# Segment means packed densely by one-hot matmuls, and two stages with longer pipelines, in a four-layer graph network kernel

## The reference

```
h   = relu(layernorm(x))                                   # layer 0
msg = concat(h[src], edge_attr_128) @ W1 + b1
m   = segment_sum(msg, dst) / max(deg, 1)
o   = m + (m @ W2 + b2);  x1 = x + where(o >= 0, o, SLOPE * o)
x2  = layer 1: attention over the edges, segment softmax by dst, batch norm, feed-forward
x3  = x2 + layer 2: gate = edge_attr_32 @ W_edge, gated messages summed per destination or source
out = x3 + layer 3: one weight per edge type, mean per (dst, type), segment_sum
```

## Time and profile before

| what | value |
| --- | --- |
| median of 3 runs | 6724.53 us (6719.76 to 6727.48) |
| the profiled execution | 6720.99 us |
| its span | 6719.2 us |
| busy: GpSimd (POOL), VectorE (DVE), TensorE (PE), ScalarE (ACT) | 66%, 61%, 58%, 34% of the span |
| data moved by DMA | 872.41 MB, 130 GB/s over the span |

### The profile page before, as it was taken

One profiled execution on the slowest core, in us unless ns is written; L12 is line 12 of the kernel. 1 busy time (PEld: TensorE's weight loads), 2 busy tenths in 40 slices (PEclk: granted clock), 3 DMA queues, 4 the chain that ended last, 5 costly groups with the idle time before them and its releaser, 6 DMA issues. The chain is left out here.

```text
span 6719.2 us, 77949 instructions
## 1 busy us (share of the span) xinstructions
PE 3919.8 (58%) x14034; PEld 2340.2 (35%) x14034; DVE 4127.0 (61%) x11066; ACT 2269.6 (34%) x4611; POOL 4404.5 (66%) x3737
## 2 busy tenths in 40 slices
PE   1666664000577777658966667777720048788776
PEld 1444442000344444434445544444410013333332
DVE  7333333676688888674455566666659976666664
ACT  1333333333344344335556521111123332222222
POOL 2777776777677777600057756666665568888887
PEclk9777677555787788758977778888865568888888
DMA  7444444887222222195467755555546633333333
GB/s 225 118 122 123 127 131 142 268 261 248 66 55 59 60 64 65 56 401 173 153 220 231 227 141 102 104 102 101 104 117 212 213 108 43 43 44 43 43 43 37
DMA packets 767166, 872.41 MB, mean 130 GB/s; under 512 B 212895, under 2 KB 425587, under 8 KB 767105
## 3 DMA queue, kind: packets, MB, share of 16 engines
q1 hardware_dynamic: 440656, 453.86, 23.5%
q0 software_dynamic: 200704, 185.92, 15.4%
q10 hardware_dynamic: 125744, 231.99, 9.3%
HBM read 452.69 MB, written 464.35 MB: 136 GB/s over the span
## 5 line engine op out<-in xcount | busy, mean ns | idle before, releaser
L544 POOL DMA_INDIRECT at_first_table<-n_h,n_first_edge x784 | 811.7, 1035 | 826.2 <-ACT n_h L226 588.0
L552 POOL DMA_INDIRECT sum_table<-e_res,e_target x392 | 660.1, 1684 | 382.1 <-DMA sum_table<-e_res,e_target 116.7
L1961 PE MATMUL e_m<-e_by_rel,rel_w 128*128 128x512 f32 x1568 | 808.6, 675 | 0.0
L552 POOL DMA_INDIRECT out<-e_res,e_target x392 | 619.4, 1580 | 133.8 <-issue 107.5
L1090 PE MATMUL e_hs<-ident,e_hs 128*128 128x128 f32 x392 | 92.8, 380 | 825.4 <-DMA e_hs<-h_table,e_idx 825.4
L544 POOL DMA_INDIRECT att_table<-e_res,e_row x392 | 461.7, 1178 | 138.8 <-issue 138.8
L536 POOL DMA_INDIRECT e_x<-x,e_idx x392 | 379.4, 968 | 241.4 <-DMA e_idx<-idx 122.1
L536 POOL DMA_INDIRECT e_hs<-h_table,e_idx x392 | 410.0, 1046 | 131.7 <-issue 119.2
L1961 PEld LDWEIGHTS e_m<-e_by_rel,rel_w 128*128 128x128 f32 x1568 | 331.4, 217 | 427.0 <-issue 427.0
L1898 DVE SCALAR_TENSOR_TENSOR e_by_rel<-e_y,e_part_t 128x512 f32<-128x512 f32 x784 | 477.5, 680 | 0.0
L544 POOL DMA_INDIRECT mean_table<-e_res,e_row x392 | 390.6, 996 | 119.5 <-issue 107.0
(11 more groups left out here) (242 smaller groups left out, 10690.0 us busy)
## 6 DMA issues: line engine op xcount, KB each, us to landing
x_table<-n_x ACTq DMA_DIRECT2D x294, 256.0 KB, 3.0
e_hd<-at_first_table SPq DMA_DIRECT2D x196, 256.0 KB
n_x<-x_table SPq DMA_DIRECT2D x196, 256.0 KB
mean_table<-prep_zero ACTq DMA_DIRECT2D x1, 25284.0 KB
n_mean<-mean_table SPq DMA_DIRECT2D x98, 258.0 KB
e_edge<-edge128T SPq DMA_DIRECT2D x98, 256.0 KB
at_first_table<-e_zero SPq DMA_DIRECT2D x98, 256.0 KB, 2.1
gate_table<-e_gate ACTq DMA_DIRECT2D x98, 256.0 KB
```

Source lines behind the costliest of these rows:

```text
L544: pool.indirect_dma_start(out=table, out_offset=bass.IndirectOffsetOnAxis(ap=idx[:, t:t + 1], axis=0), in_=tile[:, t, :], in_offset=None, ...
L552: pool.indirect_dma_start(out=table, out_offset=bass.IndirectOffsetOnAxis(ap=idx[:, t:t + 1], axis=0), in_=tile[:, t, :], in_offset=None, ...
L1961: ins = pe.matmul(flat(at(ps_m, u - 1)), k.rel_w[:, r, :], at(by_rel, u - 1)[:, r, :], start=(r == 0), stop=(r == RELS - 1))
```

## The change

Layer 0's table of means is no longer indexed by node. Each run of equal `dst` has a number; the table `mean_runs` holds one row of 130 numbers for each run, in order: the mean, the first edge's position and the destination. In e0 a one-hot matrix (`pick`, made by comparing a run's place inside its half step with 1 to 256) is multiplied with the 512 rows of results, so that the last edge of each run lands at its run's row (`ps_c`); ScalarE copies the 512 packed rows out, and SyncE writes them by two plain DMAs of 256 rows at a row number that it reads from a table. Rows behind the last run are rubbish that the next write covers, so each of these writes waits until the one before has landed. The scatter by GpSimd, and the zeros in `mean`, are gone.

In n0, SyncE loads for each tile of 128 nodes the 128 rows of `mean_runs` that begin with the first run of that tile; VectorE compares each row's destination with the node numbers (`local`, `pick`), and four matmuls spread the rows to their nodes. `prepare` computes run numbers and row numbers (a small search with a gather), folds W2 + 1 into W1 and b1 (so L704 becomes a transposition), and rewrites the indices, since node tables now hold a step's rows in another order (row p of tile t at 4p + t). The zeros of `att` are written in e0 by SyncE instead of in n0 by ScalarE. The gate is computed in e2, where it is used, and no more stored. The output of n4 goes out in natural order, in runs of 512 bytes. Both stages are rewritten with a tile's step on each engine one body later, so that e0 has tiles of 12 to 17 steps in work. The diff, cut to its core:

```diff
...
+def starts_of(nc, k, i, col, n):
+    _, values = nc.values_load_multi_w_load_instructions(
+        k.starts[0:1, bass.ds(i, 1), col:col + n].rearrange("a s c -> a (s c)"), engines=(SP,), min_val=0,
+        max_val=k.last_start)
+    return values
...
+            sp.wait_ge(places_made, 1)
+            sp.dma_start(scratch["idx"], idx_placed[:, :]).then_inc(stored, 16)
+            sp.dma_start(scratch["keys"], keys_placed[:, :]).then_inc(stored, 16)
+            sp.wait_ge(search_made, 1)
+            sp.dma_start(scratch["search"].rearrange("(s t) c -> s t c", t=TILES),
+                         search[:, :, :, :].rearrange("s t n p -> s t (n p)")).then_inc(search_stored, 16)
             sp.wait_ge(tables_done, 1)
+            sp.dma_start(scratch["starts"], starts_tab[:, :]).then_inc(starts_stored, 16)
...
+            sp.dma_start(k.starts[:, :, :], scratch["starts"].rearrange("(a s) c -> a s c", a=1)).then_inc(starts_in, 16)
+            sp.wait_ge(starts_in, 16)
...
-            act.dma_start(scratch["mean"].rearrange("(p r) d -> p (r d)", p=P).rearrange("p (s c) -> p s c", s=S),
-                         zero[:, :].unsqueeze(1).broadcast_to([P, S, TILES * MEAN_COLS])).then_inc(zeroed, 16)
...
+            for n, part, placed in ((idx_all, idx_part, idx_placed), (keys, keys_part, keys_placed)):
+                dve.tensor_scalar(placed[:, :], n[:, :], P - 1, 2, ALU.bitwise_and, ALU.logical_shift_left)
+                done(dve.tensor_scalar(part[:, :], n[:, :], 7, TILES - 1, ALU.logical_shift_right, ALU.bitwise_and))
+                done(dve.tensor_tensor(placed[:, :], placed[:, :], part[:, :], ALU.add))
+                done(dve.tensor_scalar(part[:, :], n[:, :], 9, 9, ALU.logical_shift_right, ALU.logical_shift_left))
+                done(dve.tensor_tensor(placed[:, :], placed[:, :], part[:, :], ALU.add))
+            dve.sem_inc(places_made, 1)
...
+            done(dve.tensor_copy(heads[:, :], heads_i[:, :]))
+            for t in range(TILES):
+                done(dve.tensor_scalar(below[:, :], heads[:, :], block_first[0:S, t:t + 1], None, ALU.is_lt))
+                done(dve.tensor_tensor_reduce(spare[:, :], below[:, :], below[:, :], 1.0, 0.0, ALU.mult, ALU.add,
+                                              ahead[:, t:t + 1]))
+            dve.tensor_scalar(part_i[0:S, :], ahead[:, :], -1.0, 0.0, ALU.add, ALU.max).then_inc(part_made, 1)
+            done(dve.tensor_tensor_scan(runs[:, :], first[:, :], none[:, :], 0.0, ALU.add, ALU.add))
...
+            def place_half(j, u, begins, h):
+                if not (isinstance(j, int) and j == 0 and h == 0):
+                    sp.wait_ge(placed, (j * HALVES + h) * 16)
+                sp.dma_start(run_rows(scratch["mean_runs"], begins[2 * h], HALVES),
+                             at(packed, u)[:, HALVES * h:HALVES * h + HALVES, :]).then_inc(placed, 16)
...
+                w = i - 16
+                if live(w, S):
+                    begins = starts_of(nc, k, w, 0, TILES)
+                    sp.wait_ge(packed_ready, w + 1)
+                    place_half(w, u, begins, 0)
...
                     sp.dma_start(rows_of(scratch["at_first"], i), zero[:, :]).then_inc(at(zeroed, u), 16)
+                    sp.dma_start(rows_of(scratch["att"], i), zero[:, :]).then_inc(at(zeroed, u), 16)
+                if live(w, S):
+                    place_half(w, u, begins, 1)
             sp.wait_ge(zero_ready, 1)
-            run_steps(sp, body, S, 1)
+            run_steps(sp, body, S, 16, 20)
             for u in range(SLOTS):
-                sp.wait_ge(zeroed[u], all_moved(S, u))
+                sp.wait_ge(zeroed[u], all_moved(S, u, 2))
+            sp.wait_ge(placed, HALVES * 16 * S)
...
-                j = i - 4
-                if live(j, S):
-                    pool.wait_ge(res_ready, j + 1)
-                    pool.sem_inc(pool_turn, 1)
-                    scatter(pool, scratch["mean"], at(res, u), at(row, u), size.rows - 1, at(scattered, u))
...
+                j = i - 9
+                if live(j, S):
+                    dve.wait_ge(at(row_in, u - 9), moved(j, u - 9))
+                    if begun(j - 2):
+                        dve.wait_ge(pack_done, j - 1)
+                    for t in range(TILES):
+                        wide = P * (1 + t % HALVES)
+                        ins = dve.tensor_scalar(at(pick, u - 9)[:, t // HALVES, P * (t % HALVES):P * (t % HALVES) + wide],
+                                                k.place_row[:, 0:wide],
+                                                at(row, u - 9)[:, LAST_SLOT * TILES + t:LAST_SLOT * TILES + t + 1].bitcast(F32),
+                                                None, ALU.is_equal)
+                    ins.then_inc(pick_ready, 1)
+                    dve.tensor_copy(at(res, u - 9)[:, :, D:RUN_COLS].rearrange("p t n -> p n t"),
+                                    at(row, u - 9)[:, FIRST_EDGE * TILES:(DST + 1) * TILES].bitcast(F32).rearrange(
+                                        "p (n t) -> p n t", t=TILES))
+                    dve.wait_ge(out_done, j + 1)
+                    dve.tensor_tensor(at(res, u - 9)[:, :, 0:D], at(ps_r, u - 9)[:, :, :],
+                                      spread(values(at(row, u - 9), INV_DEG), D), ALU.mult).then_inc(res_ready, 1)
...
+                j = i - 11
+                if live(j, S):
+                    act.wait_ge(pack_done, j + 1)
+                    if begun(j - 4):
+                        act.wait_ge(placed, (j - 3) * HALVES * 16)
+                    for b in range(HALVES):
+                        ins = act.activation(at(packed, u - 11)[:, HALVES * b:HALVES * b + HALVES, :], ps_c[b][:, :, :],
+                                             ACT.Copy)
+                    ins.then_inc(packed_ready, 1)
...
+                        ins = pe.transpose(at(ps_r, u - 8)[:, t, :], at(run, u - 8)[:, t * P:(t + 1) * P], k.ident[:, :])
...
+                j = i - 10
+                if live(j, S):
+                    pe.wait_ge(res_ready, j + 1)
+                    pe.wait_ge(pick_ready, j + 1)
+                    if begun(j - 1):
+                        pe.wait_ge(packed_ready, j)
+                    for b in range(HALVES):
+                        low, high = HALVES * b, HALVES * b + 1
+                        pe.matmul(ps_c[b][:, 0, :], at(pick, u - 10)[:, b, 0:P], at(res, u - 10)[:, low, :], start=True,
+                                  stop=False)
+                        pe.matmul(ps_c[b][:, 0, :], at(pick, u - 10)[:, b, P:2 * P], at(res, u - 10)[:, high, :],
+                                  start=False, stop=True)
+                        ins = pe.matmul(ps_c[b][:, 1, :], at(pick, u - 10)[:, b, 2 * P:3 * P],
+                                        at(res, u - 10)[:, high, :], start=True, stop=True)
+                    ins.then_inc(pack_done, 1)
+            run_steps(pe, body, S, 10, 16)
...
+                    begins = starts_of(nc, k, i, TILES, TILES)
+                    if begun(i - 4):
+                        sp.wait_ge(mean_done, i - 3)
+                    for t in range(TILES):
+                        sp.dma_start(at(mean, u)[:, t, :], scratch["mean_runs"][bass.ds(begins[t], P), :]
+                                     ).then_inc(at(mean_in, u), 16)
...
+                    for t in range(TILES):
+                        ins = pe.matmul(at(ps_m, u - 1)[t // HALVES][:, t % HALVES, :], at(pick, u - 1)[:, t, :],
+                                        at(mean, u - 1)[:, t, 0:D + 1], start=True, stop=True)
+                    ins.then_inc(mean_done, 1)
...
+                    dve.wait_ge(mean_done, j + 1)
+                    for b in range(HALVES):
+                        half = slice(HALVES * b, HALVES * b + HALVES)
+                        ins = dve.tensor_scalar(at(absent, u)[:, half], at(ps_m, u)[b][:, :, D], 0.5, FAR, ALU.is_lt,
+                                                ALU.mult)
+                    ins.then_inc(absent_ready, 1)
+                    if begun(j - 2):
+                        dve.wait_ge(leaky_ready, j - 1)
+                    for b in range(HALVES):
+                        half = slice(HALVES * b, HALVES * b + HALVES)
+                        ins = dve.tensor_tensor(at(biased, u)[:, half, :], at(ps_m, u)[b][:, :, 0:D],
+                                                k.b2_rep[:, half, :], ALU.add)
+                    ins.then_inc(biased_ready, 1)
+                    dve.wait_ge(absent_ready, j + 1)
+                    for b in range(HALVES):
+                        half = slice(HALVES * b, HALVES * b + HALVES)
+                        ins = dve.scalar_tensor_tensor(
+                            k.first_edges[:, bass.ds(j, 1), half].rearrange("p a t -> p (a t)"), at(ps_m, u)[b][:, :, D],
+                            -1.0, at(absent, u)[:, half], ALU.add, ALU.add)
+                    ins.then_inc(kept_ready, 1)
...
+                    dve.sem_inc(copy_turn, 1)
```

(24 more changed lines are left out.)

498 lines of the change are left out of this document (291 added, 207 removed).

## The result

The changed kernel takes 6498.11 us (median of four executions: three of 6494.53 to 6500.28, and a disturbed one of 12,813.6 us that the ratio leaves out) against 6722.15 us before on the same chip: ratio 0.9666 [0.9647, 0.9685], 3.3% faster. The forecast was 6440, with 6330 to 6580 for 8 in 10. The profiled execution has a span of 6498.5 us against 6719.2 before.

What follows compares the result with a forecast made beforehand. GpSimd bounded e0 and n0 before; e0's chain of writes would bound it after. 6721.0 + 25 (prepare) - 340 (e0) + 30 (n0) + 3 (output) = 6439, median 3.5 above, said as 6440; range 6330 to 6580 for 8 in 10.

Steps and rivals of the forecast that it cites:

- prepare** +25: Prepare stage: added VectorE work of 22.5 us and 2.5 us at the end make it 25 us longer, 15 to 35.
- The forecast's chain: e0: each half's write waits for the landing before it; 6.4 us a step, above every engine; stage 678 us, -340.
- L: e0: landing time of a half's write, taken as 3.0 us, bounds 2.1 and 4.3; a step is 3.4 + L.
- the loads of four registers: e0, SyncE: hidden under the landing; each would have to take 0.6 us before the four outlast it.
- e0, first rival: Chain hides under GpSimd's 5.3 us a step in e0; stage 588 us, total 6350; chance 0.2.
- n0** +30: n0: GpSimd's scatters stay the bound at 5.75 us a step; stage 30 us longer, 0 to +100.
- the slope: n0: GpSimd's DMA instruction, 0.997 us with VectorE a third busy, 1.089 at two thirds, reaches 1.16 at 0.9.
- The 13 us for four more bodies: n0: four more bodies before the first scatter add 13 us, part of the +30.
- the second rival: n0 turns to VectorE, or VectorE's instructions hinder GpSimd; 7 us a step, total 6540; chance 0.18.
- e2** 0: e2: the chain of adds sets the step of 10.6 us, added TensorE and ScalarE work stays inside; 0 to +30.
- the gate's 256 KB load becomes 64 KB: e2: smaller load, with four more TensorE products (0.9 us) and a ScalarE copy (0.6 us), priced at 0 us.
- e1: A stage of the kernel, not a run; forecast to read the same bytes as before, so a change of 0 us.

Runs made afterwards that it cites:

- zeros_late: Changed kernel with both stores of zeros in e0 issued behind the second half's write instead of ahead of it; 6550.67 us, ratio 0.9736.
- own_rows: Changed kernel with each half written to rows of its own, so no write waits for another, register loads kept; 6456.61 us, ratio 0.9598.
- two_regs: Changed kernel, SyncE loading two of four starts, one call each; 7047.91 us, ratio 0.9691 on another chip; repeated where kernel before took 6721.73: 6491.46 us, ratio 0.9653.
- b_gate_e2: Kernel before with only the gate moved from e0 into e2, SyncE's waits as in the changed kernel; 7313.14 us, ratio 1.0065, on another chip.
- best2: Changed kernel with att's zeros in n0, two register loads, e2's feature load also waiting for VectorE's product, at_first's zeros in prepare; 6360.81 us, ratio 0.9462.

## Why the prediction was right, and where not

**prepare** +25: as forecast; VectorE's busy time makes 19 of it (102.86 to 122.05 us), where the working had 22.5.

**e0, the bound.** The forecast's chain is the bound that it said, and the engines lie below it as it said (VectorE 4.4 us a step, ScalarE 3.5, GpSimd 5.0 to 5.1 when it is let). The size was off by 39 us. L was taken as 3.0 and is 3.07, which is close. But either gap is 3.4 us on average: the one from first to second half was priced at 3.25, and on the landing the forecast put 0.15 us where the trace has some 0.3. A step of 6.85 instead of 6.4 makes 37 us, the first placement at 74 us instead of 68 another 6, and the rest of the stage is some 2 us shorter than summed. The step that "the loads of four registers" lie under the landing, because each would have to take 0.6 us to outlast it, is right by a hair: together they take 1.70 us, and with the issues of the write and of idx that fills the gap to within 0.01 us of the landing. With a shorter landing they would have kept the step near the same length, so the term needed both prices.

The Trainium skill (DMA: Bandwidth & Descriptors, Anatomy of one DMA) gives a fixed 2.0 us and the bytes at 436 GB/s, for DMAs issued by GpSimd, while these are SyncE's; for such a write that is an estimate of 2.3 us. The medians of the runs lie above it, 2.7 us in zeros_late and 3.5 in own_rows, beside much other traffic. The Trainium skill (Runtime: NRT & Kernel Launch, Instruction fetch mechanics) puts a register load at some 200 ns a register. The load of four took 0.6 us here, 0.15 each, so the trace agrees in size; what the forecast left out is the 0.26 us that each value takes behind it. By the Trainium skill's 2.3 us the step would have been under 6, an estimate; the rows of before, taken as bounds, were nearer.

**e0, first rival** (GpSimd keeps the pace): not so here, but true once chain and loads are gone (546.3 us).

**n0** +30: measured -10. The step that failed is the slope: that GpSimd's DMA instruction grows with VectorE's busy share. VectorE went from 0.67 to 0.83 of the stage, and the scatter from 1.089 to 1.027 us. What lengthens a scatter is to overlap n_leaky or n_x, and in the new order of work this cost 0.12 us a time instead of 0.25, nearly as often (128 of 339, 122 of 288); why it costs less was not settled. The 13 us for four more bodies were nearly right (11).

So VectorE does get in the way of GpSimd's instructions, as the second rival had it, but not more than before: n0 did not turn to VectorE, and in e0 the gathers that overlap the copy, comparisons or product of the new part take 0.98 to 0.99 us against 0.95 for the others, 0.961 on average. The Trainium skill's rule on the shared port pair (SBUF — State Buffer, Who interferes with whom) names VectorE's fast modes and, against a GpSimd instruction that reads SBUF, its operations with two inputs in SBUF. n_leaky and n_x agree with that; the 85 scatters that n_pick did not lengthen do not. The zeros are not the reason (555.1 with them back, scatters at 1.028). On the other chip the sign turns: there n0 took 692.1 us in two_regs against 608.6 with the code of before in b_gate_e2, and VectorE waited 72.6 us for the new loads of `mean_runs`, 1020 to 1600 us. The forecast had set these loads against the zeros.

**e2** 0: measured +65. The argument asked whether the added work of TensorE and ScalarE reaches the path, and it does not. What it did not ask is what the removed load had held back. The failed step is "the gate's 256 KB load becomes 64 KB": the load's wait changed with it, from VectorE's product to TensorE's, and with it the moment at which keys and hd, next in SyncE's queue, leave. That was to be read in the diff and in SyncE's waits of before.

**The total.** +39 in e0, -40 in n0, +65 in e2, and under 5 in the rest: two misses cancelled by luck, and the third, with small differences, is the 58 us between forecast and result. That the result lies in the range owes something to that.

## What to carry to other kernels

When a load is replaced, look at the wait that stood before it: it also timed everything behind it in that queue, and transfers that leave earlier can delay the one whose landing is the path. Before a chain of landings is called the bound, add up the whole queue of the engine that issues it, register loads included: when two limits are equally long, removing one shows little. Before a run is taken as a test, see in its trace that the edit took out what it was to take out; two_regs did not. Do not price an engine's slowdown by how busy another one is; look at which instructions overlap. Stores that only prepare memory belong in a stage where the queues idle, whichever that is.

## What the runs showed of the hardware

- To load four row numbers from SBUF into SyncE's registers and check them took 1.70 us of its queue a step: one load of 0.6 us and 0.26 us for each value. Two calls for one value each took 1.67 us. The engine table and the timeline do not list it; the view of the line does.
- A write of 130 KB in rows of 520 bytes landed after 2.7 us (median, in zeros_late) or 3.5 us (in own_rows) with stores of zeros and gathers beside it, and after 2.5 to 2.7 us with the zeros gone (best2).
- A scatter's instruction on GpSimd took 0.98 us, and 1.23 us on average (before) where it overlapped a VectorE instruction with two 128x512 float32 inputs in SBUF (n_leaky, n_x); n_pick, equally long, did not lengthen it.
- With two 256 KB loads issued around the last of four indirect adds it landed after 4.0 us instead of 3.3, and the stage took 58 us longer over 98 steps.
- On one chip the stages e0, n0, e1 and n2 (`second_norm_nodes`) were longer in every kernel profiled there: for b_gate_e2 1195.2, 608.6, 1281.5 and 681.3 us, where the kernel before had 1020.6, 564.6, 1142.8 and 525.3. n1, which moves 389 GB/s in the kernel before, kept its 198.7 us, so it does not look like plain bandwidth; I have no explanation.
